# Moving the output clearings, the stores' steps and the sign copies around the sigmoid sets of a WKV and binary-FFN kernel

## The chip, the cores and the metric

The kernel runs on one core of a Trainium2 chip. The metric is device time of one launch in microseconds (us). The engines are called PE (TensorE), DVE (VectorE), ACT (ScalarE), POOL (GpSimd) and SP (SyncE); a "line" such as L963 is a line of the kernel before.

## What is computed

For x and k of shape (4, 1024, 1024), batch, time, channel:

```
ek = exp(min(k, 30)); ekv = ek * k
forward and backward scans over time, with a decay per channel and batch, of ekv and of ek
den = df + db - ek + exp(min(u + k, 30));  num likewise with ekv
out = sigmoid(x) * num / max(den, 1e-8) * (0.8 + 0.2 * tf)
y   = out @ (sign(weight) * mean|weight|).T + bias
result = x + y
```

tf is a sigmoid of the sum of a batch's condition row.

## The kernel before, in words

**Tiles and steps.** The work is cut into N = 32 tiles, one per batch and group of 128 channels, each 128 channels by 1024 times in float32. There are 32 steps, n = 0 to 31; every engine has its own program with a `step(n, ...)` of its own, and semaphores tie them together. LAST is 24 (the last batch's first tile), SOON is 26 and LAG is 9.

**One tile's way through the engines.** PE turns k and x into channel-major form (`k_turn`, `s_turn`). ACT makes the exponentials (`exps`, L655 to L659). DVE multiplies (L939, L942), scans four times (L911 forward twice, L925 backward twice), adds up the denominator (L963, both tensor inputs in SBUF), and forms `gate` of the tile before (L954: wkv times sigmoid). The reciprocal takes a chain over two engines: ACT `inverse` (L690, L692), POOL L379 (semaphore `chk`), ACT L755 (`two`), POOL L385 (`inv`). DVE's gate of step n waits for `inv` of tile n-1. POOL multiplies the gated value with the numerator (`base`, L362), ACT splits it in a high and a low half (`halves`, L699 and L701), and POOL L342 writes the low half (`lo`) that PE's products use. POOL's order in a step is base(n-2), a store if one is due, chk(n-1), lo(n-2), inv(n-1), the numerator's accumulating DMA L388, and at step 28 and later a second store if one is due.

**Sigmoid sets.** Sigmoids need another activation table, so ACT does three x tiles at once in every third step (L796, with a table load before and after, L796 and L802). Six further x tiles lie in `x_end`; before, one of them is done in each sigmoid step from 9 on (L801).

**Products, clearings and stores.** For the first three batches an output tile m is made in two halves, unit u = 2m and 2m+1, of 16 matmuls each (`unit`, L466). ACT clears a unit from PSUM (`evac`, L669), PE turns it back to time-major form (`turned`, L468), and ACT copies it into one of four buffers `o_nat[m % 4]` (`y_copy`, L678). `clear(lo, hi)` does `evac(u)` and `y_copy(u-1)` for its units. POOL then adds tile m to the output with an accumulating DMA (`store`, L355). `y_copy(2m)` waits until `store(m-4)` has landed, since it writes the same buffer:

```
if h == 0 and m >= NO:
    act.wait_ge(o_out[m % NO], m // NO * 16)
```

**Two tables set the order.** `made(n)` says how many units PE has made by step n (`MORE` holds exceptions), `cleared(n)` how many ACT has cleared (`CLEARED` holds exceptions). From `cleared` follows the step of every store: one step after its second half is copied, one store per step, two from step 28 on:

```
n = copied[2 * m + 1] + 1
while added.count(n) >= (2 if n >= N - 4 else 1) or added and n < added[-1]:
    n += 1
```

**A step right behind a sigmoid set** (n % 3 == 1, up to 22) is "hasty": ACT does the halves before any clearing. In steps 0 to 7 ACT also prepares the weight's signs (absolute sum, sign, and the copy into `sgn`, L806). From step 26 on PE does `s_turn` first; steps 30 and 31 and the tail do the last batch in time-major form (`begun`, `across`, L488), with the results scaled on DVE (L1025 to L1035).

## Time and profile before

| | us |
|---|---|
| median of 3 runs | 514.82 |
| lowest and highest run | 514.12 and 516.09 |
| the profiled execution's own time | 513.96 |
| its span in the trace | 512.1 |
| VectorE busy | 482.4 (94%) |
| ScalarE busy | 411.1 (80%) |
| GpSimd busy | 381.1 (74%) |
| TensorE matmul busy | 354.7 (69%) |

The span is the trace's own length; the execution's time has 1.9 us more around it. All places below are given in us from the span's start. A busy engine is not yet a bound engine: an instruction that is held up inside counts as busy.

### The profile page before, as it was taken

The numbers are of one execution on the slowest core, as the hardware profiler recorded it, in microseconds if no ns is written. First come the engines' busy times: TensorE is split into PE (matmuls) and PEld (weight loads), VectorE is DVE, ScalarE is ACT, GpSimd is POOL, SyncE is SP. The second block draws the span as 40 slices with busy tenths as digits, with TensorE's granted clock in tenths as the row PEclk, the third lists the DMA queues.
The fourth block names the chain that finished last, engine by engine and source line by source line (L and its number), as shares of the span: only waits on it lengthen the run. The fifth ranks groups of instructions, "written<-read, shape, count | busy, mean of one in ns | idle before, by whom it ended". The sixth has DMA issues, their size and how long they took to land.

```text
span 512.1 us, 5399 instructions
## 1 busy us (share of the span) xinstructions
PE 354.7 (69%) x1803; PEld 209.6 (41%) x1803; DVE 482.4 (94%) x346; ACT 411.1 (80%) x459; POOL 381.1 (74%) x210
## 2 busy tenths in 40 slices
PE   3322223332288876877688698788849999999996
PEld 2212222332244443444254354355425555544442
DVE  6999998999999999999999999989999999999666
ACT  3978998898889879988988988898698888894500
POOL 0067769848777886888689678869778889999483
PEclk9996656555687998889898889979788999999999
DMA  8877999999997989598798957879866559995368
GB/s 216 228 213 241 256 224 234 293 314 242 265 245 188 204 194 165 142 200 190 161 199 190 205 83 209 162 164 206 165 114 90 108 102 150 193 153 78 42 113 217
DMA packets 101283, 94.22 MB, mean 184 GB/s; under 512 B 2924, under 2 KB 93064, under 8 KB 100744
## 3 DMA queue, kind: packets, MB, share of 16 engines
q0 software_dynamic: 31440, 36.18, 46.1%
q1 hardware_dynamic: 67720, 56.65, 35.1%
q10 hardware_dynamic: 2096, 1.05, 0.8%
q8 instruction: 15, 0.25, 0.2%
q14 instruction: 12, 0.10, 0.1%
HBM read 60.31 MB, written 37.75 MB: 191 GB/s over the span
## 4 chain that ended last, share of the span: by engine, by line
POOL 23%; ACT 23%; PE 22%; issue 16%; DVE 14%; DMA 0%; SPq 0%; DVEq 0%; ACTq 0%; POOLq 0%
POOL wkv L379 9%; PE prod L447 8%; DVE terms L925 4%; POOL acts L342 4%; DVE terms L911 4%; POOL wkv L385 4%; POOL out_dram L355 3%; PE prod L488 3%; ACT x_nat L796 3%; ACT rec L690 2%; ACT terms L655 2%; ACT euk L659 2%; ACT rec L692 2%; PE sT L488 2%; PE kT L488 2%
## 5 line engine op out<-in xcount | busy, mean ns | idle before, releaser
L447 PE MATMUL prod<-acts,sgn 128*128 128x512 f16 x752 | 180.2, 395 | 0.0
L925 DVE TENSOR_TENSOR_SCAN terms<-cols,y_start,terms 128x1024 f32<-128x1024 f32 x64 | 147.0, 2337 | 1.1
L911 DVE TENSOR_TENSOR_SCAN terms<-cols,terms 128x1024 f32<-128x1024 f32 x64 | 142.7, 2270 | 0.0
L447 PEld LDWEIGHTS prod<-acts,sgn 128*128 128x128 f16 x752 | 76.7, 102 | 86.6 <-issue 13.5
L362 POOL TENSOR_TENSOR wkv<-wkv,terms 128x1024 f32<-128x1024 f32 x31 | 73.4, 2367 | 50.7 <-DVE wkv L954 50.7
L379 POOL TENSOR_TENSOR wkv<-euk,rec 128x1024 f32<-128x1024 f32 x31 | 82.3, 2654 | 37.2 <-ACT rec L692 37.2
L385 POOL TENSOR_TENSOR wkv<-wkv,rec 128x1024 f32<-128x1024 f32 x31 | 81.8, 2639 | 1.2 <-ACT wkv L755 1.2
L342 POOL TENSOR_TENSOR acts<-wkv,rec 128x1024 f16<-128x1024 f32 x30 | 77.7, 2590 | 4.7 <-ACT rec L701 4.6
L422 PE MATMUL prod<-ident,o_nat 128*128 128x128 f16 x64 | 8.3, 311 | 72.8 <-ACT o_nat L790 72.8
L422 PE MATMUL kT<-ident,k_nat 128*128 128x128 f32 x248 | 45.9, 347 | 16.7 <-DVE own L942 16.5
L422 PE MATMUL sT<-ident,x_nat 128*128 128x128 f32 x208 | 38.0, 343 | 25.4 <-DVE wkv L954 16.7
L963 DVE SCALAR_TENSOR_TENSOR euk<-euk,terms 128x1024 f32<-128x1024 f32 x31 | 52.8, 1704 | 1.1
L755 ACT ACTIVATE wkv<-wkv 128x1024 f32<-128x1024 f32 x31 | 32.7, 1055 | 23.6 <-POOL wkv L379 23.6
L422 PE MATMUL yT<-ident,y_fm 128*128 128x128 f32 x192 | 31.2, 288 | 26.2 <-ACT o_nat L678 25.7
L388 POOL DMA_DIRECT2D terms<-own x32 | 35.8, 1120 | 17.4 <-DVE terms L925 17.2
L422 PEld LDWEIGHTS kT<-ident,k_nat 128*128 128x128 f32 x248 | 38.7, 184 | 23.7 <-issue 22.7
L422 PEld LDWEIGHTS sT<-ident,x_nat 128*128 128x128 f32 x208 | 31.3, 179 | 28.8 <-issue 16.3
L954 DVE SCALAR_TENSOR_TENSOR wkv<-wkv,sT 128x1024 f32<-128x1024 f32 x31 | 37.6, 1212 | 4.6 <-POOL wkv L385 4.6
L669 ACT ACTIVATE y_fm<-prod,bcol,oscale 128x512 f32<-128x512 f32 x47 | 36.1, 769 | 4.8 <-PE prod L447 2.7
L355 POOL DMA_DIRECT2D out_dram<-o_nat x24 | 39.9, 1662 | 0.0
L422 PEld LDWEIGHTS yT<-ident,y_fm 128*128 128x128 f32 x192 | 23.8, 148 | 38.9 <-ACT y_fm L669 32.7
L690 ACT ACTIVATE rec<-euk,lnb 128x1024 f32<-128x1024 f32 x31 | 35.7, 1151 | 4.5 <-DVE euk L963 4.4
(119 smaller groups left out, 587.0 us busy)
## 6 DMA issues: line engine op xcount, KB each, us to landing
terms<-own POOLq DMA_DIRECT2D x32, 512.0 KB, 5.2
out_dram<-in_x_dram SPq DMA_DIRECT2D x32, 512.0 KB, 7.2
k_nat<-in_fside_BxSxS_dram SPq DMA_DIRECT2D x30, 512.0 KB, 6.1
x_nat<-in_x_dram SPq DMA_DIRECT2D x26, 512.0 KB, 3.6
out_dram<-o_nat POOLq DMA_DIRECT2D x24, 512.0 KB, 8.0
y_fm<-in_L_ffn_weight_dram SPq DMA_DIRECT2D x8, 512.0 KB, 8.0
out_dram<-in_L_ffn_bias_dram POOLq DMA_DIRECT2D x8, 512.0 KB, 7.5
x_end<-in_x_dram SPq DMA_DIRECT2D x6, 512.0 KB, 8.9
```

The source lines that it names most:

```text
L342: pool.tensor_tensor(acts[:, 1, n % (2 * CT), :], wkv[p][:, :], rec[p][:, :], ALU.subtract)\
L355: pool.dma_start(tile_of(out, m), o_nat[m % NO][:, :, :], accum_op=ALU.add)\
L362: pool.tensor_tensor(wkv[n % 2][:, :], wkv[n % 2][:, :], ekv[n % NV], ALU.mult).then_inc(st["base"], 1)
L379: pool.tensor_tensor(W, euk[1 - p][:, :], R, ALU.mult).then_inc(st["chk"], 1)
L385: pool.tensor_tensor(W, W, R, ALU.mult).then_inc(st["inv"], 1)
L422: ins = pe.transpose(dst(q), what(q), one)
L447: ins = pe.matmul(made_in(u), view[:, c, m % CT * P:m % CT * P + P], acts[:, part, m // CT % 2 * CT + c, h * H:(h + 1) * H], start=(part = ...
L690: act.activation(rec[p][:, :], euk[p][:, :], ACT.Ln, bias=lnb[:, 0:1]).then_inc(st["ln"], 1)
L911: dve.tensor_tensor_scan(buf, d, buf, 0.0, ALU.mult, ALU.add).then_inc(st["F" + kind], 1)
L925: dve.tensor_tensor_scan(buf[:, ::-1], d, buf[:, ::-1], y_start[:, i:i + 1], ALU.mult, ALU.add)\
L954: dve.scalar_tensor_tensor(W, W, HI_SCALE * LO_GAIN / DEN_MIN, sT[:, :], ALU.min, ALU.mult)\
L963: dve.scalar_tensor_tensor(U, U, E30, E, ALU.min, ALU.add).then_inc(st["den"], 1)
```

## The change

Five things change. (1) In a sigmoid step from 9 to 21 only one unit is cleared (none in step 9); the other is cleared in the next step. `MORE` and `CLEARED` say so, and in such a step PE leaves out the last `turned` and does it in the next step, behind `k_turn`. (2) One unit more is made in steps 20 and 23, and one less in steps 19 and 22. (3) The copy of unit 31 (step 24) stands behind `two` instead of ahead of the halves. (4) The sign copy of step n moves to step n+1, behind `two`. (5) Of the six sigmoids in `x_end`, two are done in step 9 and one each in steps 12 to 21 (before, one each in steps 9 to 24), and their loads are issued in steps 2 to 7 instead of 4 to 9.

```diff
-    MORE = {19: 23, 20: 25, 21: 28, 22: 30, 23: 32, 24: 32, 25: 36, 26: 39, 27: 42, 28: 45}
+    MORE = {20: 25, 21: 27, 22: 29, 23: 32, 24: 32, 25: 36, 26: 39, 27: 42, 28: 45}
...
-    CLEARED = {23: 32, 25: 35, 26: 38, 27: 41, 28: 44, 29: 47}
+    CLEARED = {9: 0, 12: 6, 15: 12, 18: 18, 21: 25, 23: 32, 25: 35, 26: 38, 27: 41, 28: 44, 29: 47}
...
+    def turns(n):
+        return n % 3 == 0 and n < SOON
...
-                if 4 <= n < 10:
-                    sp.dma_start(x_of(SOON + n - 4), tile_of(x, SOON + n - 4)).then_inc(s_soon, 16)
+                if 2 <= n < 8:
+                    sp.dma_start(x_of(SOON + n - 2), tile_of(x, SOON + n - 2)).then_inc(s_soon, 16)
...
+                if turns(n - 1) and LAG < n < LAST:
+                    turned(units[0] - 2)
...
-                    turned(u - 1)
+                    if not turns(n):
+                        turned(u - 1)
...
-                hasty = low and n < LAST and n % 3 == 1
+                hasty = low and n < LAST and turns(n - 1)
...
-                if n == LAST:
-                    y_copy(4 * CT - 1)
                 if late and n < N - 2 and not hasty:
                     clear(cleared(n - 1), sooner)
...
+                if n == LAST:
+                    y_copy(4 * CT - 1)
                 if late and hasty:
                     clear(cleared(n - 1), sooner)
+                if 1 <= n <= CT:
+
+                    done(act, "wT", n - 1)
+                    act.mul(sgn[:, :, (n - 1) * P:n * P], wT, SIGN).then_inc(st["wTc"], 1)
...
-                    if n >= 9:
+                    for i in {9: (0, 1), 12: (2,), 15: (3,), 18: (4,), 21: (5,)}.get(n, ()):
 
                         act.wait_ge(s_soon, 16 * (N - SOON))
-                        i = SOON + n // 3 - 3
-                        act.activation(x_of(i), x_of(i), ACT.Sigmoid).then_inc(st["soon"], 1)
+                        act.activation(x_of(SOON + i), x_of(SOON + i), ACT.Sigmoid).then_inc(st["soon"], 1)
...
-                if wt:
-
-                    done(act, "wT", n)
-                    act.mul(sgn[:, :, n * P:(n + 1) * P], wT, SIGN).then_inc(st["wTc"], 1)
```

Evaluated, the two tables give these clearings and stores (steps that differ, and the last ones):

| step | cleared before | cleared now | store before | store now |
|---|---|---|---|---|
| 12 | 5, 6 | 5 | 1 | 1 |
| 13 | 7, 8 | 6, 7, 8 | 2 | none |
| 14 | 9, 10 | 9, 10 | 3 | 2 |
| 19 | 19, 20, 21 | 18, 19, 20 | 8 | 7 |
| 23 | 29, 30, 31 | 28, 29, 30, 31 | 12 | 11 |
| 27 | 38, 39, 40 | 38, 39, 40 | 16 | 15 |
| 28 | 41, 42, 43 | 41, 42, 43 | 17, 18 | 16, 17 |
| 29 | 44, 45, 46 | 44, 45, 46 | 19, 20 | 18, 19 |
| 30 | 47 | 47 | 21, 22 | 20, 21 |
| 31 | none | none | 23 | 22, 23 |

**First place: ScalarE, end of step 12 and start of step 13.** In the names a digit is a buffer's number; L669 is `evac`, L678 `y_copy`, L690 and L692 the `inverse` of tile 12. Before:

```order
L659 ACTIVATE euk1<-kT,ucol 128x1024
L669 ACTIVATE y_fm1<-prod,bcol,oscale 128x512
L678 COPY o_nat2<-yT 128x512
L796 ACT_TABLE_LOAD
L796 ACTIVATE x_nat0<-x_nat0 128x1024
L796 ACTIVATE x_nat1<-x_nat1 128x1024
L796 ACTIVATE x_nat2<-x_nat2 128x1024
L801 ACTIVATE x_end<-x_end 128x1024
L802 ACT_TABLE_LOAD
L690 ACTIVATE rec0<-euk0,lnb 128x1024
L692 ACTIVATE rec0<-rec0 128x1024
```

Now:

```order
L665 ACTIVATE euk1<-kT,ucol 128x1024
L806 ACT_TABLE_LOAD
L806 ACTIVATE x_nat0<-x_nat0 128x1024
L806 ACTIVATE x_nat1<-x_nat1 128x1024
L806 ACTIVATE x_nat2<-x_nat2 128x1024
L810 ACTIVATE x_end<-x_end 128x1024
L811 ACT_TABLE_LOAD
L696 ACTIVATE rec0<-euk0,lnb 128x1024
L698 ACTIVATE rec0<-rec0 128x1024
```

One clearing (two instructions) has left the place ahead of the table load; it stands in step 13 now, behind `exps`.

**Second place: GpSimd, from base(25) to the second store of step 28.** o_nat0 to o_nat3 are the four output buffers; tile m lies in buffer m % 4. Before:

```order
L362 TENSOR_TENSOR wkv1<-wkv1,terms 128x1024 [waits num_in1,d_gate]
L355 DMA out_0_dram<-o_nat0 128x8x128 [waits x_out2,d_yc]
L379 TENSOR_TENSOR wkv0<-euk0,rec0 128x1024 [waits d_lo,d_rec]
L342 TENSOR_TENSOR acts<-wkv1,rec1 128x1024 [waits d_hib]
L385 TENSOR_TENSOR wkv0<-wkv0,rec0 128x1024 [waits d_two]
L388 DMA terms<-own1 128x1024 [waits d_yn]
L362 TENSOR_TENSOR wkv0<-wkv0,terms 128x1024 [waits num_in0,d_gate]
L355 DMA out_0_dram<-o_nat1 128x8x128 [waits x_out2,d_yc]
L379 TENSOR_TENSOR wkv1<-euk1,rec1 128x1024 [waits d_lo,d_rec]
L342 TENSOR_TENSOR acts<-wkv0,rec0 128x1024 [waits d_hib]
L385 TENSOR_TENSOR wkv1<-wkv1,rec1 128x1024 [waits d_two]
```

Now, from base(26) on:

```order
L365 TENSOR_TENSOR wkv0<-wkv0,terms 128x1024 [waits num_in0,d_gate]
L358 DMA out_0_dram<-o_nat0 128x8x128 [waits x_out2,d_yc]
L382 TENSOR_TENSOR wkv1<-euk1,rec1 128x1024 [waits d_lo,d_rec]
L345 TENSOR_TENSOR acts<-wkv0,rec0 128x1024 [waits d_hib]
L388 TENSOR_TENSOR wkv1<-wkv1,rec1 128x1024 [waits d_two]
L391 DMA terms<-own0 128x1024 [waits d_yn]
L358 DMA out_0_dram<-o_nat1 128x8x128 [waits x_out2,d_yc]
L365 TENSOR_TENSOR wkv1<-wkv1,terms 128x1024 [waits num_in1,d_gate]
L358 DMA out_0_dram<-o_nat2 128x8x128 [waits x_out2,d_yc]
```

The store of o_nat0 (tile 16) has moved from step 27 to step 28, behind base(26), and that of o_nat1 (tile 17) from the start of step 28 to its end.

**Third place: ScalarE, start of step 28.** The same instructions before and now; those now are:

```order
L696 ACTIVATE rec1<-euk1,lnb 128x1024 [waits d_lo,d_den]
L698 ACTIVATE rec1<-rec1 128x1024 [waits d_ln]
L675 ACTIVATE y_fm0<-prod,bcol,oscale 128x512 [waits d_yT,d_prod,s_osc]
L684 COPY o_nat0<-yT 128x512 [waits d_yT,o_out0]
L705 ACTIVATE acts<-wkv0 128x1024 [waits d_prod,d_base]
```

The copy of unit 40 into o_nat0 (semaphore o_out0: tile 16's store has landed) stands ahead of the halves of tile 26, unmoved by the change.

## Rows read from the trace of the kernel before

**Rows 1.** Busy time of each engine: us (share of span), instructions.
```profile
PE 354.7 (69%) x1803; PEld 209.6 (41%) x1803; DVE 482.4 (94%) x346; ACT 411.1 (80%) x459; POOL 381.1 (74%) x210
```
**Rows 2.** Groups of instructions, DVE: xcount, busy us, mean ns, idle us before.
```profile
L963 DVE SCALAR_TENSOR_TENSOR euk<-euk,terms 128x1024 f32<-128x1024 f32 x31 | 52.8, 1704 | 1.1
```
**Rows 3.** What DVE waited for: us in total, times, longest.
```profile
DVE wkv L954 <- POOL wkv L385: 4.6, 3, 2.2
```
**Rows 4.** DVE's timeline, steps 4 to 22: start us, us.
```profile
75.37 1.72 DVE L963 SCALAR_TENSOR_TENSOR euk<-euk,terms 128x1024 f32<-128x1024 f32 x1
79.33 1.22 DVE L954 SCALAR_TENSOR_TENSOR wkv<-wkv,sT 128x1024 f32<-128x1024 f32 x1 [2.24 <-POOL wkv L385]
...
193.37 1.23 DVE L963 SCALAR_TENSOR_TENSOR euk<-euk,terms 128x1024 f32<-128x1024 f32 x1
...
207.29 3.28 DVE L963 SCALAR_TENSOR_TENSOR euk<-euk,terms 128x1024 f32<-128x1024 f32 x1
...
310.92 2.86 DVE L963 SCALAR_TENSOR_TENSOR euk<-euk,terms 128x1024 f32<-128x1024 f32 x1
...
344.78 1.22 DVE L954 SCALAR_TENSOR_TENSOR wkv<-wkv,sT 128x1024 f32<-128x1024 f32 x1 [2.25 <-POOL wkv L385]
```
**Rows 5.** POOL's timeline, steps 13 and 20.
```profile
202.51 2.35 POOL L379 TENSOR_TENSOR wkv<-euk,rec 128x1024 f32<-128x1024 f32 x1 [2.78 <-ACT rec L692]
...
207.14 2.34 POOL L385 TENSOR_TENSOR wkv<-wkv,rec 128x1024 f32<-128x1024 f32 x1
...
308.01 2.38 POOL L342 TENSOR_TENSOR acts<-wkv,rec 128x1024 f16<-128x1024 f32 x1 [1.42 <-ACT rec L701]
```
**Rows 6.** ACT's timeline, steps 3 and 12.
```profile
68.12 1.02 ACT L806 ACTIVATE sgn<-prod 128x1024 f16<-128x1024 f16 x1
...
192.42 0.77 ACT L669 ACTIVATE y_fm<-prod,bcol,oscale 128x512 f32<-128x512 f32 x1
...
193.68 1.28 ACT L796 ACT_TABLE_LOAD   x1
```
**Rows 7.** PE's timeline, steps 13 and 14.
```profile
208.12 4.71 PE L447 MATMUL prod<-acts,sgn 128*128 128x512 f16 x16
...
218.90 3.62 PE L447 MATMUL prod<-acts,sgn 128*128 128x512 f16 x16
```
**Rows 8.** POOL's timeline, steps 28 and 29.
```profile
419.81 1.59 POOL L355 DMA_DIRECT2D out_dram<-o_nat  x1
...
429.14 1.90 POOL L355 DMA_DIRECT2D out_dram<-o_nat  x1
```
**Rows 9.** ACT's timeline, step 28: inverse, copies of units 40 and 42.
```profile
419.26 1.06 ACT L692 ACTIVATE rec<-rec 128x1024 f32<-128x1024 f32 x1
...
421.21 0.58 ACT L678 COPY o_nat<-yT 128x512 f32<-128x512 f32 x1
...
430.97 0.58 ACT L678 COPY o_nat<-yT 128x512 f32<-128x512 f32 x1
```
**Rows 10.** DMA issues at 419 to 421: xcount, KB each, us to landing.
```profile
out_dram<-o_nat POOLq DMA_DIRECT2D x1, 512.0 KB, 6.3
```
**Rows 11.** DMA issues at 429 to 430, the same columns.
```profile
out_dram<-o_nat POOLq DMA_DIRECT2D x1, 512.0 KB, 8.2
```
**Rows 12.** Landing times of all transfers from or to o_nat.
```profile
DMA to landing us min/median/max: 6.0/8.0/11.5
```
**Rows 13.** DMA issues of the whole page, the plain x loads.
```profile
x_nat<-in_x_dram SPq DMA_DIRECT2D x26, 512.0 KB, 3.6
```
**Rows 14.** DVE's timeline, steps 28 and 30: L963 and two gates.
```profile
428.96 1.22 DVE L963 SCALAR_TENSOR_TENSOR euk<-euk,terms 128x1024 f32<-128x1024 f32 x1
430.11 1.21 DVE L954 SCALAR_TENSOR_TENSOR wkv<-wkv,sT 128x1024 f32<-128x1024 f32 x1
...
457.95 1.21 DVE L954 SCALAR_TENSOR_TENSOR wkv<-wkv,sT 128x1024 f32<-128x1024 f32 x1
```
**Rows 15.** ACT's timeline, step 30: the first parked result.
```profile
452.60 0.57 ACT L706 COPY acts<-prod 128x512 f32<-128x512 f32 x1
```

More of the change, by code:

```diff
@@ L791, in step @@
                        .then_inc(st["sgn"], 1)
-                if n % 3 == 0 and n < SOON:
+                if turns(n):
                     for i in range(n, min(n + 3, SOON)):
```

## The prediction, made blind

> **What bounds the kernel now.** I read the engines' busy time first. VectorE is busy 482.4 of 512.1 us [rows 1], so nothing is gained that doesn't shorten VectorE's own sequence. But the groups of instructions show that part of this is no work: L963 takes 1704 ns in the mean of its 31 [rows 2], and 1.23 us where nothing disturbs it [rows 4]. 31 times (1.704 - 1.225) is 14.8 us. The waits add 4.6 us for L954 (`gate`) behind GpSimd's L385 (`inv`) [rows 3].
>
> The timelines say where it goes. From one free L963 to the next it is 207.29 - 193.37 = 13.92 us [rows 4]. At 207.29 L963 takes 3.28, and GpSimd's L385 had begun at 207.14 and ran until 209.48 [rows 5]: L963, which reads two SBUF tensors, finished 1.09 after L385's end. So a step loses (end of L385) - (start of L963) - 0.13, here 2.06. In step 4 L385 came later still; there L963 took 1.72 and the gate waited 2.24 [rows 4], 2.8 us in all. All such losses together are 14.8 + 4.6 = 19.4 us, and that is the most that any cure of them can bring. They lie in the steps behind sigmoid sets (4, 7, 10, 13, 16, 19, 22), in step 20 (2.86 - 1.23 = 1.6 [rows 4]) and, with under 1 us each, in 24, 25 and 27. L385 is late since ScalarE is: L379 waited 2.78 us for `rec` [rows 5], which stands behind the sigmoids and table loads.
>
> For the rest the useful measure is the distance from a gate to L385. The next L963 starts 1.15 + 11.6 = 12.8 us after a gate starts; L385 takes 2.34 [rows 5], so it does no harm if it starts within 10.4 us of the gate.
>
> **The change, part by part.**
>
> *The clearing that leaves the sigmoid step.* From 192.42 to 193.68 it holds ScalarE 1.26 us [rows 6]. Without it `rec`, L379 and L385 all come 1.26 earlier: L385 ends at 208.22, and step 13 loses 0.8 instead of 2.06. Steps 13, 16 and 19: -3.8. In step 10 one more sigmoid of about 0.95 comes in for the clearing, so -0.3. Step 22 also gets rid of the clearing behind its sigmoid set: -2.0 of its 3.2 (its gate waited 2.25 [rows 4]).
>
> *What the following steps get for it.* In step 13 the turning of unit 6 now waits for its `evac` behind `two`. PE has idled over 5 us by then; the unit at 208.12, behind an idle of 3.6, took 4.71, the warm one at 218.90 took 3.62 [rows 7]. I take 4.7 for unit 8 and put it at 206.3 to 210.9. ScalarE has three units to clear in that step, waits for unit 8, and begins `inverse` of tile 13 at 212.1, some 3 us after its denominator. In step 14 it waits again, for unit 9 (214.8), then come the halves (to 218.1), L342 (to 220.5), L385: 11.2 us behind the gate, 0.8 too late. That is what step 20 shows already: L342 at 308.01 waited 1.42 for L701 [rows 5]. So 0.7 to 0.8 is newly lost in each of steps 11, 14, 17 and 23: +2.9. Step 20, which had this loss at 1.6, keeps 0.7: -0.9.
>
> *Units moved to 20 and 23.* In step 23 PE now has three units; unit 31 ends about 19.2 us after the gate, its clearing pushes `inverse` of tile 23 some 5.9 us back, and step 24 loses 2.2 instead of 0.9: +1.3. Unit 31's copy behind `two`, and one sigmoid less in step 24, save the small losses of 25 and 27: -0.5.
>
> *Sign copies.* One takes 1.02 us [rows 6] and leaves the place ahead of `inverse`. But it now delays `exps` in the step before a set, where ScalarE is held to GpSimd's base and L379, so the set starts later by as much. -0.75 in step 4, -0.1 in step 7.
>
> *Loads of x_end two steps earlier.* Used 90 us later: 0; at worst they push k's loads, +1.
>
> Sum up to step 27: -3.8 -0.3 -2.0 +2.9 -0.9 +1.3 -0.5 -0.75 -0.1 = **-4.2 us**. From above it is bounded by -19.4, from below by 0 if the new waits take back all.
>
> *The stores.* Step 13 has no store now, and one per step is the rule, so every later tile is stored a step later up to step 28. Up to unit 38 a copy into o_nat finds its store landed. Unit 40 doesn't. Store 16 is issued at 419.81 [rows 8], the slot of store 17 before, and that slot's transfer lands after 6.3 [rows 10]: 426.1. The copy of unit 40 stood at 421.21 [rows 9]. Queued behind it on ScalarE are the halves, `two`, `exps`. In the frame of before:
>
> - 426.1, copy 0.5, halves twice 1.1 (ScalarE's pass of 1024 is 1.06 [rows 9]): 428.8. L342 2.3, then L385, which is held up by the L963 that began at 428.96 [rows 14] as the one of step 4 was, 3.3: 434.5. The gate stood at 430.11 [rows 14]: +4.4.
> - Store 17 now follows L385 and L388: issued at 434.5 + 0.6 = 435.1, landing 8.2 as in the same slot [rows 8, 11]: 443.3. The copy of unit 42 stood at 430.97 [rows 9] and has `inverse` of tile 28 behind it. 443.3 + 0.5, inverse 2.2, clearing 1.1, halves 2.2, L342 and L385 4.7: 454.0.
> - Store 19 follows that L385: 454.6, landing 8.0 (the median [rows 12]) 462.6, copy of unit 46 and halves 2.7: 465.3; L342 2.3, L385 3.3: 470.9. The gate stood at 457.95 [rows 14]: +13.0.
> - `two` ends and the first parked copy starts at 466.3 against 452.60 [rows 15]: +13.7. PE waits for it and has the last batch's products in front of it without a pause.
>
> I take **+13.6**, and +1.0 for PE's slower matmuls after its idle stretches (4.71 - 3.62 = 1.1 once [rows 7]).
>
> Total: -4.2 + 13.6 + 1.0 = +10.4. The profiled execution took 513.96, so 524.4; the median of the runs is 0.86 above that execution: 525.2, rounded to **525**. Landings at the ends of 6.0 and 11.5 [rows 12] move the three stalls together by -4.5 and +12; the part up to step 27 by +4 and, if the new waits stay out, -5. The forecast's own range is 517 to 532.
>
> **Rivals.**
>
> *A, a store lands in time.* The plain x loads of the same 512 KB land after 3.6 us [rows 13]. If the stores did, unit 40's copy would wait 423.4 - 421.2 = 2.2, unit 42's some 2 and unit 46's nothing, +3 to +4 at the end, and with -4.2 the kernel stays at 514. For it: a plain transfer of the size does it. Against it: no transfer of o_nat landed under 6.0 [rows 12]. The Trainium skill (DMA: Bandwidth & Descriptors, section on the anatomy of one SWDGE DMA) gives about 2.0 us plus bytes over 436 GB/s; by that estimate a store would land after 3.2 us and the sum would end near 514 too. By that rule the trace disagrees, with 6.0 to 11.5 for these accumulating stores. Chance 0.09: no change.
>
> *B, faster.* The place is L963 behind L385 in steps 10 to 27. It decides itself at 10.4 us from gate to L385: if ScalarE, 1.26 us ahead at each set, stays ahead and PE doesn't hold up units 8 and 9, L385 gets in under that in every step and all of the 19.4 but the 4.2 left in steps 4 and 7 go: -15.2. With the stalls at their low end (13.6 - 4.5 = 9.1) and PE's 1.0 that is -5.1, so 510. Against: 1.26 is less than the 2.2 by which L385 must move. Chance 0.07: faster.
>
> *C, the change doesn't do what it says.* If the sets' x tiles landed late, the earlier table load would be waited away. They are loaded a step ahead and land in 3.6 [rows 13], so I see it as part of the range: +6, 531.
>
> **How the numbers follow.** Forecast and C 0.84, all slower; A 0.09; B 0.07. 0.5% (2.6 us) is about what a measurement of this kernel can tell from no change. Range 515 to 532: it leaves out B, half of A and the longest landings.
>
> **What would show it.** In the changed trace: ScalarE's copies L684 (old L678) waiting for a DMA in steps 28 and 30, three waits of 5 to 10 us in all 18 to 23; VectorE's gates of steps 28 to 30 late by 4, 10 and 13; the L963 behind steps 13, 16, 19 about 2.0 instead of 3.3, and those of 14, 17 near 2.0 instead of 1.2; the span up to step 27's L963 about 4 shorter. I am wrong if no copy waits for a store, or if the waits end without moving the gates.

## The result and the profile after

The changed kernel takes **528.45 us** (median of 4 runs, 527.65 to 530.26) against 515.46 for the kernel before on the same chip: 1.026 of its time, 95% interval 1.0223 to 1.0297. It is slower, by 13 us. The profiled execution took 530.26, with a span of 528.4 (before: 513.96 and 512.1), so in the traces the difference is 16.3 us, and that is what has to be explained below. Some 3 us of it belong to this pair of executions and not to the change: the changed kernel's profiled execution is the slowest of its four, and that of the kernel before lies 1.5 below its median.

In the changed file lines have moved: the denominator L963 is L968, the gate L954 is L959, `inv` L385 is L388, `lo` L342 is L345, `chk` L379 is L382, `base` L362 is L365, the store L355 is L358, `evac` L669 is L675, `y_copy` L678 is L684, the `inverse` is L696 and L698, the halves are L705 and L707.

Busy time of each engine in the changed kernel, beside [rows 1]:

```profile
PE 354.3 (67%) x1797; PEld 209.4 (40%) x1803; DVE 488.7 (92%) x346; ACT 411.1 (78%) x459; POOL 383.7 (73%) x210
```

The group of the denominator in the changed kernel (xcount, busy us, mean ns, idle before), beside [rows 2]:

```profile
L968 DVE SCALAR_TENSOR_TENSOR euk<-euk,terms 128x1024 f32<-128x1024 f32 x31 | 58.6, 1889 | 1.1
```

And what VectorE, ScalarE and TensorE waited for in the changed kernel (us in total, times, longest), beside [rows 3]:

```profile
PE yT L425 <- ACT o_nat L684: 35.8, 9, 8.3
...
ACT o_nat L684 <- DMA out_dram<-o_nat: 14.5, 3, 7.9
DVE wkv L959 <- POOL wkv L388: 14.1, 6, 4.6
```

The work is the same on every engine. VectorE is busy 6.3 us longer, of which the 31 denominators have 5.8 (58.6 - 52.8), and its gates wait 14.1 us instead of 4.6, another 9.5. Together that is 15.8 of the 16.3. ScalarE now waits for stores to land, 14.5 us in three waits; there was no such wait before.

**Where in the program.** The measure of the prediction, the time from one denominator to the next less 13.92 us, taken for each step of both traces from VectorE's timeline (us; steps not named lose under 0.1 in both):

| step | 4 | 7 | 10 | 11 | 13 | 14 | 16 | 17 | 19 | 20 | 22 | 23 | 24 | 25 | 26 | 27 | sum |
|---|---|---|---|---|---|---|---|---|---|---|---|---|---|---|---|---|---|
| before | 2.8 | 2.2 | 1.6 | 0 | 2.1 | 0 | 2.1 | 0 | 2.1 | 1.6 | 3.2 | 0 | 0.9 | 0.4 | 0 | 0.5 | 19.5 |
| changed | 2.3 | 2.2 | 1.4 | 2.4 | 0.9 | 2.4 | 0.9 | 2.0 | 0.9 | 1.9 | 1.0 | 1.8 | 1.9 | 0.2 | 0.2 | 1.6 | 23.8 |

Up to step 27 the changed kernel loses 4.3 us more in this pair of traces. The rest, 12.4 us, comes in steps 28 to 30: the first parked copy stands at 469.32 against 452.60 [rows 15], 16.7 later, and the last products are 16.7 later too.

**Steps 28 to 30.** ScalarE's timeline in the changed kernel, the copies of units 40, 42 and 46, and the halves behind the first (start us, us, what ended the idle time before it):

```profile
430.36 0.59 ACT L684 COPY o_nat<-yT 128x512 f32<-128x512 f32 x1 [4.76 <-DMA out_dram<-o_nat]
430.85 1.06 ACT L705 ACTIVATE acts<-wkv 128x1024 f16<-128x1024 f32 x1
...
446.91 0.59 ACT L684 COPY o_nat<-yT 128x512 f32<-128x512 f32 x1 [7.90 <-DMA out_dram<-o_nat]
...
465.83 0.59 ACT L684 COPY o_nat<-yT 128x512 f32<-128x512 f32 x1 [1.83 <-DMA out_dram<-o_nat]
```

GpSimd's timeline in the changed kernel, the stores of tiles 16, 17 and 19 and the instructions that the first wait holds up:

```profile
424.09 1.60 POOL L358 DMA_DIRECT2D out_dram<-o_nat  x1
...
433.07 2.36 POOL L345 TENSOR_TENSOR acts<-wkv,rec 128x1024 f16<-128x1024 f32 x1 [4.99 <-ACT rec L707]
435.39 3.34 POOL L388 TENSOR_TENSOR wkv<-wkv,rec 128x1024 f32<-128x1024 f32 x1
...
439.28 1.90 POOL L358 DMA_DIRECT2D out_dram<-o_nat  x1
...
458.25 1.91 POOL L358 DMA_DIRECT2D out_dram<-o_nat  x1
```

VectorE's gates of steps 28, 29 and 30 in the changed kernel, beside [rows 14]:

```profile
438.76 1.22 DVE L959 SCALAR_TENSOR_TENSOR wkv<-wkv,sT 128x1024 f32<-128x1024 f32 x1 [2.25 <-POOL wkv L388]
...
457.73 1.22 DVE L959 SCALAR_TENSOR_TENSOR wkv<-wkv,sT 128x1024 f32<-128x1024 f32 x1 [4.57 <-POOL wkv L388]
...
474.23 1.21 DVE L959 SCALAR_TENSOR_TENSOR wkv<-wkv,sT 128x1024 f32<-128x1024 f32 x1
```

Read them together. From a store's issue to the copy that waits for it is 430.36 - 424.09 = 6.3 us, then 446.91 - 439.28 = 7.6, then 465.83 - 458.25 = 7.6. The store leaves only behind `inv`, the copy stands ahead of the halves, and the halves lead to the next `inv`: each wait makes the next store late, and so the next wait.

**Steps 13 and 14.** VectorE's timeline in the changed kernel:

```profile
208.97 2.13 DVE L968 SCALAR_TENSOR_TENSOR euk<-euk,terms 128x1024 f32<-128x1024 f32 x1
211.02 1.21 DVE L959 SCALAR_TENSOR_TENSOR wkv<-wkv,sT 128x1024 f32<-128x1024 f32 x1
...
223.80 1.23 DVE L968 SCALAR_TENSOR_TENSOR euk<-euk,terms 128x1024 f32<-128x1024 f32 x1
227.28 1.22 DVE L959 SCALAR_TENSOR_TENSOR wkv<-wkv,sT 128x1024 f32<-128x1024 f32 x1 [2.26 <-POOL wkv L388]
```

TensorE's timeline in the changed kernel, the held-back turning of unit 6 and the products of units 8 and 9:

```profile
207.76 1.09 PE L425 MATMUL yT<-ident,y_fm 128*128 128x128 f32 x4 [6.01 <-ACT o_nat L684]
208.64 5.56 PE L450 MATMUL prod<-acts,sgn 128*128 128x512 f16 x16
214.03 0.60 PE L425 MATMUL yT<-ident,y_fm 128*128 128x128 f32 x4
214.47 3.62 PE L450 MATMUL prod<-acts,sgn 128*128 128x512 f16 x16
```

ScalarE's timeline there in the changed kernel: the held-back clearing, the wait for unit 8, the `inverse` of tile 13:

```profile
206.38 0.76 ACT L675 ACTIVATE y_fm<-prod,bcol,oscale 128x512 f32<-128x512 f32 x1
207.04 0.57 ACT L684 COPY o_nat<-yT 128x512 f32<-128x512 f32 x1
...
214.28 0.78 ACT L675 ACTIVATE y_fm<-prod,bcol,oscale 128x512 f32<-128x512 f32 x1 [2.26 <-issue]
214.96 0.58 ACT L684 COPY o_nat<-yT 128x512 f32<-128x512 f32 x1
215.43 1.16 ACT L696 ACTIVATE rec<-euk,lnb 128x1024 f32<-128x1024 f32 x1
```

GpSimd's timeline in step 14 of the changed kernel:

```profile
221.55 2.37 POOL L345 TENSOR_TENSOR acts<-wkv,rec 128x1024 f16<-128x1024 f32 x1 [1.42 <-ACT rec L707]
223.88 3.37 POOL L388 TENSOR_TENSOR wkv<-wkv,rec 128x1024 f32<-128x1024 f32 x1
```

The profile puts ScalarE's wait of 2.26 to `issue`, which means that it shows no releaser; the unit that is cleared next ended on TensorE at 214.20, 0.1 us before.

Behind the sigmoid set the denominator takes 2.13 instead of 3.28 [rows 4], which is the gain of the change. In the next step `inv` starts at 223.88, 12.9 us behind the gate of 211.02, and the gate after it waits 2.26. The loss has moved one step on, and grown: 0.9 + 2.4 for steps 13 and 14 against 2.1 before.

**How far one trace can be read.** The changed kernel and e1 below are the same program up to step 19, and still step 11 loses 2.4 in the one and 1.5 in the other, and step 14 2.35 and 1.89. TensorE's timeline, the first products of step 10, in the changed kernel and in e1:

```profile
163.00 6.18 PE L450 MATMUL prod<-acts,sgn 128*128 128x512 f16 x16
...
163.09 5.33 PE L450 MATMUL prod<-acts,sgn 128*128 128x512 f16 x16
```

The granted clock is 0.58 over the first and 0.68 over the second, the products end 0.9 us apart, and so does everything behind them. In step 13 the products take 5.56 and 5.14. In the same way step 10 of e2, which lies ahead of its only edit, loses 2.5 where the kernel before loses 1.6. So a difference of up to 1 us in one step of two traces need not come from an edit. The larger ones, and those that stand in several runs, can be read.

### The profile page after: what moved, and what is told of

Same layout as the page of the kernel before. It is cut to its first block, busy times and chain, and to the rows that moved or that the text cites. A ratio compares the mean times of both kernels' runs of the same rounds, so it can differ in the third digit from the quotient of the medians.

```text
span 528.4 us, 5393 instructions
## 1 busy us (share of the span) xinstructions
PE 354.3 (67%) x1797; PEld 209.4 (40%) x1803; DVE 488.7 (92%) x346; ACT 411.1 (78%) x459; POOL 383.7 (73%) x210
## 4 chain that ended last, share of the span: by engine, by line
PE 29%; ACT 28%; POOL 16%; issue 13%; DVE 9%; DMA 4%; SPq 0%; ACTq 0%; DVEq 0%; POOLq 0%
PE prod L450 15%; POOL wkv L382 7%; DMA out_dram<-o_nat 4%; POOL wkv L388 4%; ACT x_nat L806 3%; PE prod L491 3%; DVE terms L930 3%; PE yT L425 3%; DVE terms L916 2%; ACT terms L661 2%; ACT rec L696 2%; ACT euk L665 2%; ACT L811 2%; ACT L806 2%; POOL acts L345 2%
## 5 line engine op out<-in xcount | busy, mean ns | idle before, releaser
L450 PE MATMUL prod<-acts,sgn 128*128 128x512 f16 x752 | 182.7, 399 | 0.0
L365 POOL TENSOR_TENSOR wkv<-wkv,terms 128x1024 f32<-128x1024 f32 x31 | 75.5, 2435 | 50.5 <-DVE wkv L959 50.5
L382 POOL TENSOR_TENSOR wkv<-euk,rec 128x1024 f32<-128x1024 f32 x31 | 79.5, 2565 | 39.2 <-ACT rec L698 39.1
L345 POOL TENSOR_TENSOR acts<-wkv,rec 128x1024 f16<-128x1024 f32 x30 | 73.9, 2464 | 17.5 <-ACT rec L707 17.3
L388 POOL TENSOR_TENSOR wkv<-wkv,rec 128x1024 f32<-128x1024 f32 x31 | 80.1, 2583 | 1.2 <-ACT wkv L759 1.2
L968 DVE SCALAR_TENSOR_TENSOR euk<-euk,terms 128x1024 f32<-128x1024 f32 x31 | 58.6, 1889 | 1.1
L425 PE MATMUL kT<-ident,k_nat 128*128 128x128 f32 x248 | 43.8, 335 | 16.3 <-DVE own L947 16.3
L675 ACT ACTIVATE y_fm<-prod,bcol,oscale 128x512 f32<-128x512 f32 x47 | 36.3, 772 | 21.6 <-issue 14.6
L425 PE MATMUL sT<-ident,x_nat 128*128 128x128 f32 x208 | 36.0, 330 | 24.8 <-ACT x_nat L806 16.8
L959 DVE SCALAR_TENSOR_TENSOR wkv<-wkv,sT 128x1024 f32<-128x1024 f32 x31 | 37.6, 1213 | 14.1 <-POOL wkv L388 14.1
L425 PEld LDWEIGHTS yT<-ident,y_fm 128*128 128x128 f32 x192 | 25.0, 152 | 52.8 <-ACT y_fm L675 35.6
L391 POOL DMA_DIRECT2D terms<-own x32 | 31.8, 994 | 17.2 <-DVE terms L930 17.1
L684 ACT COPY o_nat<-yT 128x512 f32<-128x512 f32 x48 | 27.8, 579 | 19.3 <-DMA out_dram<-o_nat 14.5
L358 POOL DMA_DIRECT2D out_dram<-o_nat x24 | 41.1, 1740 | 1.3 <-ACT o_nat L684 1.3
```

The source lines that it names most:

```text
L345: pool.tensor_tensor(acts[:, 1, n % (2 * CT), :], wkv[p][:, :], rec[p][:, :], ALU.subtract)\
L358: pool.dma_start(tile_of(out, m), o_nat[m % NO][:, :, :], accum_op=ALU.add)\
L365: pool.tensor_tensor(wkv[n % 2][:, :], wkv[n % 2][:, :], ekv[n % NV], ALU.mult).then_inc(st["base"], 1)
L382: pool.tensor_tensor(W, euk[1 - p][:, :], R, ALU.mult).then_inc(st["chk"], 1)
L388: pool.tensor_tensor(W, W, R, ALU.mult).then_inc(st["inv"], 1)
L425: ins = pe.transpose(dst(q), what(q), one)
```

## The experiments

Each is set against the kernel before on the same chip (medians of before: 515.58 for e1 to e4, 514.91 for f5 to f8, 515.18 for g1 to g4). Runs of different groups ran on different chips and are compared by these ratios.

| run | what it is | median us | ratio to before, 95% |
|---|---|---|---|
| changed kernel | | 528.45 | 1.026 (1.0223 to 1.0297) |
| e1 | changed, stores back in their steps | 516.52 | 1.001 (0.9993 to 1.0028) |
| e2 | before, stores late only | 528.04 | 1.0239 (1.0218 to 1.026) |
| e3 | e1, eviction ahead of the halves | 512.78 | 0.9945 (0.9926 to 0.9965) |
| e4 | before with parts 3, 4, 5 | 513.78 | 0.9972 (0.9957 to 0.9986) |
| f5 | e1, whole clearing ahead of the halves | 509.33 | 0.9887 (0.9856 to 0.9918) |
| f6 | e1, unit 29 back in step 22 | 517.04 | 1.0038 (1.0019 to 1.0056) |
| f7 | e4, low half behind `inv` | 512.73 | 0.9943 (0.9925 to 0.996) |
| f8 | e3, low half behind `inv` | 513.91 | 0.9979 (0.9957 to 1.0001) |
| g1 | f5, low half behind `inv` in steps 4, 7 | 508.99 | 0.9877 (0.9853 to 0.99) |
| g2, g3, g4 | before with part 4, 3 or 5 alone | 514.88, 514.40, 514.49 | one run each |

### The stores: taken out of the change, and put alone into the kernel before

e1 is the changed kernel with room for two stores in step 20, so that every store from tile 9 on has the step it had before:

```diff
-        while added.count(n) >= (2 if n >= N - 4 else 1) or added and n < added[-1]:
+        while added.count(n) >= (2 if n >= N - 4 or n == 20 else 1) or added and n < added[-1]:
```

> The changed kernel with one edit: two stores may be issued in step 20, so that from tile 9 on every store is in the step where it was before. Theory S (the one-step delay of the stores makes ScalarE's copies wait in steps 28 and 30, which the trace after shows as 14.5 us of DMA waits and 12.0 us more between VectorE's step 27 and the last gate): the waits vanish, and about 12 us with them: 516 to 519 us, the DVE steps up to 27 as in the changed kernel. Rival R (the copies of steps 28 to 30 would be late in any case, since ScalarE and TensorE come out of step 27 late): the time stays above 523 us, with other waits in place of the DMA's.

e2 is the kernel before with the stores of tiles 2 to 16 a step late and nothing else:

```diff
-        n = copied[2 * m + 1] + 1
+        n = max(copied[2 * m + 1] + 1, m + 12 if 2 <= m <= 16 else 0)
```

> The kernel before with one edit: stores 2 to 16 are issued one step later, as in the changed kernel; clearings, products and sign copies are as before. Theory S: the same three DMA waits, 526 to 529 us. Rival R (the delay hurts only in company with the other parts): under 521 us.

Measured: e1 516.52, no difference from before that can be told; e2 528.04, the changed kernel's time to half a microsecond. What ScalarE's copies waited for in e2:

```profile
ACT o_nat L678 <- DMA out_dram<-o_nat: 15.1, 4, 8.1
```

and its first two waits, on ScalarE's timeline:

```profile
427.89 0.59 ACT L678 COPY o_nat<-yT 128x512 f32<-128x512 f32 x1 [4.87 <-DMA out_dram<-o_nat]
...
444.63 0.59 ACT L678 COPY o_nat<-yT 128x512 f32<-128x512 f32 x1 [8.08 <-DMA out_dram<-o_nat]
```

In e1 these waits are gone. VectorE's timeline in e1, steps 28 to 30, for the rows of [rows 14]:

```profile
431.66 1.22 DVE L968 SCALAR_TENSOR_TENSOR euk<-euk,terms 128x1024 f32<-128x1024 f32 x1
432.81 1.21 DVE L959 SCALAR_TENSOR_TENSOR wkv<-wkv,sT 128x1024 f32<-128x1024 f32 x1
...
459.50 1.22 DVE L968 SCALAR_TENSOR_TENSOR euk<-euk,terms 128x1024 f32<-128x1024 f32 x1
```

459.50 - 431.66 is 27.84, two steps of 13.92 without a loss. So the stores' late steps cost 12 us in the medians, taken away (528.45 - 516.52 = 11.9) as well as added alone (528.04 - 515.58 = 12.5). This is shown, from both sides.

### What the other parts do together

e4 is the kernel before with the sign copies, unit 31's copy and the last sigmoids and their loads as in the change, but with its own clearings, units and stores (parts 3 to 5 of the diff above).

> The kernel before with the three parts of the change that don't touch the clearings' tables: sign copies a step later behind two, unit 31's copy behind two, and the x_end sigmoids and loads as in the changed kernel. Theory: the sign copies give 0.5 us in step 4 (2.83 before, 2.33 after) and nothing in step 7; unit 31's copy gives 0.9 us in step 24; the x_end sigmoids cost 1 us in step 10 and give 1 us or less in steps 24 and 25: together 1 us faster than before, 514 to 515 us. Rival (the sign copies' place carries what the change gains): 511 to 513 us.

Measured 513.78, ratio 0.9972: 1.4 us faster by the ratio, 1.8 by the medians. e1 has all five parts and the stores in place, and takes 516.52. What lies between, 2.7 us, is the price of parts 1 and 2 together, the clearings and the units, with the later stores of tiles 2 to 8 that follow from them. The clearings were meant to leave the sigmoid step, and apart from the stores they cost more than they bring.

### The held-back turning

Two theories stood for why the loss comes back a step later: the turning of the held-back unit, ahead of the products on TensorE, makes unit 8 late, and with it ScalarE's `inverse`; or ScalarE simply has as much to do as before, and the place matters little. e3 does the eviction ahead of the halves and leaves the copy behind `two`:

```diff
                 hasty = low and n < LAST and turns(n - 1)
+                if late and hasty:
+                    evac(cleared(n - 1))
                 if hasty:
...
-                if late and hasty:
-                    clear(cleared(n - 1), sooner)
+                if late and hasty and n > LAG + 1:
+                    y_copy(cleared(n - 1) - 1)
```

> The stores' cure of the run with stores moved back, and in each step behind a sigmoid set ScalarE clears the waiting unit (evac alone) ahead of the halves instead of behind the activation called two; the copy that goes with it stays behind. Theory M (the changed kernel's new losses of 1.8 to 2.4 us in steps 11, 14, 17, 20 and 23 come from the turning that TensorE holds back until that evac, and from the slow clock after its idle time): TensorE goes on some 4 us earlier, these five steps lose 0 to 1 us each, and the run is 6 to 10 us faster than the one with stores moved back alone: 508 to 512 us. Rival (the losses come from three clearings in one step, wherever they stand): 515 to 519 us, no gain over that run.

Measured 512.78, 3.7 us less than e1: a gain, and less of one than expected. TensorE's timeline in e3, the same turning:

```profile
205.18 1.08 PE L425 MATMUL yT<-ident,y_fm 128*128 128x128 f32 x4 [5.47 <-ACT o_nat L684]
206.06 4.74 PE L450 MATMUL prod<-acts,sgn 128*128 128x512 f16 x16
```

It still waits for the copy of unit 5: the turning writes `yT`, which that copy reads, and the copy (204.47, 0.57 us) now came last, 3 us behind the eviction. Counted from the denominator of step 12, the turning starts 12.2 us behind it against 12.7 in the changed kernel and in e1, so only 0.5 us sooner. f5 therefore takes the whole clearing, eviction of unit 6 and copy of unit 5, ahead of the halves:

```diff
+                if late and hasty:
+                    clear(cleared(n - 1), sooner_of(n))
                 if hasty:
                     done(act, "base", n - 2)
                     halves(n - 2, p)
...
-                if late and hasty:
-                    clear(cleared(n - 1), sooner)
```

with `sooner_of(n)` being `min(made(n - 1), cleared(n - 1) + 1)`.

> As the run with the early eviction, but in the steps behind a sigmoid set the whole held-back clearing (evictions of cleared(n-1) and the copy of unit cleared(n-1)-1) now goes ahead of the step's halves on ScalarE. Theory (the turning of the held-back unit waits for that copy too, 5.47 us in the run before, and so delays the units on TensorE): the turning starts some 3 us sooner, steps 14, 17, 20 and 23 lose about nothing instead of 0.6 to 1.1, the steps 13, 16, 19, 22 lose 1.8 instead of 1.3 since the halves come 1 us later; in all 511.5 to 512.5 us. Rival (the wait for the copy is hidden; only the halves count): 514 us or more.

Measured **509.33**, ratio 0.9887: 5.6 us faster than before, 2 us more than the theory gave; the interval is clear of no change. TensorE's timeline in f5:

```profile
202.06 0.72 PE L425 MATMUL yT<-ident,y_fm 128*128 128x128 f32 x4 [2.68 <-ACT o_nat L684]
202.57 5.26 PE L450 MATMUL prod<-acts,sgn 128*128 128x512 f16 x16
```

and VectorE's, steps 13 and 14:

```profile
206.78 3.00 DVE L971 SCALAR_TENSOR_TENSOR euk<-euk,terms 128x1024 f32<-128x1024 f32 x1
...
222.48 1.23 DVE L971 SCALAR_TENSOR_TENSOR euk<-euk,terms 128x1024 f32<-128x1024 f32 x1
```

Counted from the denominator of step 12 (192.87), the turning stands 9.2 us behind it instead of 12.7, 3.5 sooner; unit 8 is ready when ScalarE comes for it, and the denominator of step 14 is free: 1.23. Steps 14, 17, 20 and 23 lose nothing now. The price is a loss of 1.8 in step 13 again (the denominator takes 3.00), since the halves come behind the clearing. All losses up to step 27 are 15.0 us, against 19.5 before and 22.2 in e1. VectorE waits for `inv` in no step but the last, where it is 0.18. So it wasn't a matter of ScalarE's amount of work: the very same work, in another order, is 1.001 of the time before in e1 and 0.9887 in f5, some 6 us apart.

### The units of steps 22 and 23

```diff
-    MORE = {20: 25, 21: 27, 22: 29, 23: 32, 24: 32, 25: 36, 26: 39, 27: 42, 28: 45}
+    MORE = {20: 25, 21: 27, 22: 30, 23: 32, 24: 32, 25: 36, 26: 39, 27: 42, 28: 45}
```

> The changed kernel with the stores back in their former steps, and unit 29 made in step 22 again, so that step 23 makes two units and not three. Theory: the third unit of step 23 is what step 24 (1.93 us) and step 27 (1.59 us) lose by; they go to about 0.9 and 0.5, and the time from 516.5 to about 514.5. Rival: steps 22 and 23 lose as much more, since unit 29 is late in step 22 behind a held-back clearing: 516.5 us or above.

First a correction of what stands above under the change, part (2): by the table `MORE` the steps that make one unit less are 19 and 21, and not 19 and 22; step 22 makes two units in both kernels. So f6 does not restore the old table: its step 22 makes three units, 27 to 29, where before it made two, since unit 27 stays there.

Measured 517.04, no better than e1 (ratio 1.0038 against 1.001, intervals that meet); the rival had it right. VectorE's timeline in f6:

```profile
356.57 1.22 DVE L968 SCALAR_TENSOR_TENSOR euk<-euk,terms 128x1024 f32<-128x1024 f32 x1
362.36 1.22 DVE L959 SCALAR_TENSOR_TENSOR wkv<-wkv,sT 128x1024 f32<-128x1024 f32 x1 [4.57 <-POOL wkv L388]
```

Step 23 loses 4.65 instead of 1.6, and steps 24 and 25 nothing instead of 1.9 and 0.2. With unit 29 made in step 22, unit 28 is cleared in that step too, by the table. It is the second of three behind the held-back turning, and ScalarE waits 2.64 us for it ahead of the `inverse` of tile 22:

```profile
350.29 0.78 ACT L675 ACTIVATE y_fm<-prod,bcol,oscale 128x512 f32<-128x512 f32 x1 [2.64 <-issue]
...
351.43 1.16 ACT L696 ACTIVATE rec<-euk,lnb 128x1024 f32<-128x1024 f32 x1
```

In e1 the same wait of 2.64 stands one step later, for unit 31 and ahead of the `inverse` of tile 23. A third unit costs about as much in step 22 as in step 23, so this move is neither gain nor loss once part 1 is there. Part 2 without part 1 was not run.

### GpSimd's order

In f7 and f8 GpSimd makes `inv` ahead of the low half in the steps behind a sigmoid set:

```diff
-                if low:
+                behind = low and n < LAST and n % 3 == 1
+                if low and not behind:
                     low_half(n - 2, p)
                 if mid:
 
                     done(pool, "two", n - 1)
                     pool.tensor_tensor(W, W, R, ALU.mult).then_inc(st["inv"], 1)
+                if behind:
+                    low_half(n - 2, p)
```

> The kernel before with the signs, unit 31's copy and the last sigmoids as changed (513.8 us), and in the steps behind a sigmoid set GpSimd makes the reciprocal's part (wkv, L388 of the changed kernel) ahead of the low half. Theory: the gate of these steps waits 2.06 us each because that part stands last on GpSimd; with it first the loss goes to 1.1 or less in five steps, 507 to 510 us. Rival: the low half is then late for DVE's add by as much, and the step loses the same: 513 to 515 us.

> The early-eviction run (512.8 us) with the same order on GpSimd. Theory: 506 to 511 us, and the steps 13, 16, 19, 22 lose under 0.8 instead of 1.3. Rival: as in the run above, the low half is late and nothing is gained: 512 to 514 us.

Measured 512.73 and 513.91: the theory was wrong in both, and the rivals' times were right or nearly so. f7 gains 0.4 us on e4 by the medians and 1.5 by the ratios, intervals that just meet, and not 4 to 7. Its steps 13, 16 and 19 lose 1.0 instead of 2.1, as expected, but 14 and 17 now lose 1.2 where they lost nothing in the kernel before. In f8 steps 13, 16 and 19 lose nothing at all and 14, 17 and 20 lose 2.7 to 2.9. GpSimd's timeline in f8:

```profile
203.11 2.36 POOL L389 TENSOR_TENSOR wkv<-wkv,rec 128x1024 f32<-128x1024 f32 x1 [1.30 <-ACT wkv L764]
205.43 3.44 POOL L345 TENSOR_TENSOR acts<-wkv,rec 128x1024 f16<-128x1024 f32 x1
...
220.00 3.34 POOL L389 TENSOR_TENSOR wkv<-wkv,rec 128x1024 f32<-128x1024 f32 x1
```

The low half ends at 208.9 there, but unit 8's products do not wait for it: they start at 204.53, and need the low halves of tiles 0 to 7 alone. ScalarE waits 2.49 us for the unit, and the next `inv` starts at 220.00, 13.5 us behind its gate. Set beside e3, whose ScalarE and TensorE have the same order, the `inv` of step 14 starts 14.6 us behind the denominator of step 13 instead of 13.6, since unit 8's products took 5.78 us and not 4.74; and that denominator is no longer held up itself, so the gate behind it comes 1.3 us sooner. The chain over TensorE and ScalarE does not come sooner with it, and what was saved in step 13 is waited for in step 14. In the other direction the low half's lateness does show in f7: ScalarE's `inverse` waits 0.3 us for it in steps 10, 13, 16 and 22. Why f8's products were the slower ones in all three such steps (5.78, 5.64, 5.56 against 4.74, 5.12, 5.30 in e3) was not followed up.

g1 uses this order in steps 4 and 7 alone, where there are no products yet, on top of f5.

> The run with the whole clearing early (509.33 us), and GpSimd's low half behind the reciprocal's part in steps 4 and 7 alone. Where the low half was put last in all such steps, steps 4 and 7 lost 1.10 and the steps behind them 0.44, against 2.2 and nothing, a gain of 0.66 each. Theory: these two steps don't touch the rest, so 1.3 us less, 508.0 us. Rival: the order of the later steps shifts and gives it back, 509.3 us.

Measured 508.99 against f5's 509.33; the two intervals lie over each other, so the expected 1.3 us isn't there to be told. In its trace step 4 loses 1.1 and step 5 0.4, as expected, but step 7 lost 2.3 in this execution, where f8, with the same order up to there, lost 1.1.

### Parts 3, 4 and 5 one by one

Each alone in the kernel before, read by the steps' losses; the times themselves, one run each, are within 0.2% of before, which tells nothing.

> The kernel before with the signs' copies one step later and nothing else. Theory: steps 4 and 7 lose 2.2 each instead of 2.83 and 2.20, all other steps as before, 0.6 us less: the run is within 0.5% of before. Rival (the prediction's): step 4 gains 0.75 and step 7 0.1.

> The kernel before with unit 31's copy behind two turned units and nothing else. Theory: it touches only the last step, no step up to 27 loses other than before and the end moves by under 0.5 us. Rival: it is what took away the losses of steps 24 and 25 (0.91 and 0.40 us).

> The kernel before with the loads of the last x tiles two steps earlier and their sigmoids two in step 9 and one in steps 12, 15, 18 and 21. Theory: the sixth sigmoid leaves the set of step 24, so the losses of steps 24 and 25 (0.91 and 0.40) go to nothing, and comes into that of step 9, so step 10 loses 2.9 instead of 1.6: in sum nothing. Rival: step 10 stays at 1.6 and 1.3 us are gained.

| step | 4 | 7 | 10 | 20 | 22 | 24 | 25 | 27 |
|---|---|---|---|---|---|---|---|---|
| before | 2.8 | 2.2 | 1.6 | 1.6 | 3.2 | 0.9 | 0.4 | 0.5 |
| g2, signs | 2.2 | 2.2 | 2.5 | 0.5 | 3.3 | 0.9 | 0.4 | 1.4 |
| g3, copy of unit 31 | 2.8 | 2.2 | 1.6 | 1.6 | 3.3 | 0 | 0.5 | 0.8 |
| g4, last sigmoids | 2.9 | 2.2 | 2.7 | 0.5 | 3.3 | 0.9 | 0 | 0.5 |

The signs are worth 0.6 us in step 4 and nothing in step 7, as expected; every run with the signs moved and GpSimd's order left alone has 2.2 to 2.3 in step 4, every run without 2.8. The copy of unit 31 is what takes step 24's loss away, here and in e4; there the expectation was wrong and its rival right, for step 24 and not for 25. VectorE's timeline in g3:

```profile
371.44 1.23 DVE L963 SCALAR_TENSOR_TENSOR euk<-euk,terms 128x1024 f32<-128x1024 f32 x1
```

against 2.14 in the kernel before. The last sigmoids free step 25 only. Whether they bring 1.1 us into step 10 isn't shown: g2 loses 0.9 more there too, with nothing edited near it, and e2 likewise. Step 20 loses 1.1 us less in g2 and g4; the first products of step 19 took 3.6 us there and 5.3 in the kernel before and in g3. That is TensorE's pace, as above, and it is larger than the effects that are looked for.

## Why the prediction was right, and where it was not

Forecast: 525, range 515 to 532, slower with 0.84. Measured 528.45. The sign and the range hold, by the mechanism that was named. But of its two sums only one was right, and the other had the wrong sign. That the forecast came as near as 3 us is in part luck: errors of 8.5 and 2.2 us in the trace stand against each other. The direction is not luck, since the stores' 12 us alone carry it.

**The stores: right, a little high (+13.6 predicted, 12.4 in the trace, 12 by e1 and e2).** The table takes off the 4.3 us by which the changed kernel is behind when it leaves step 27, and is in the frame of before:

| | predicted | measured |
|---|---|---|
| landing of store 16, then the copy's wait | 6.3, 4.9 | 6.3, 4.76 |
| gate of step 28 | +4.4 | 438.76 - 4.3 - 430.11 = +4.3 |
| store 17 issued | 435.1 | 439.28 - 4.3 = 435.0 |
| issue to copy, store 17 | 8.2 | 7.6 |
| end of `inv` in step 29 | 454.0 | 455.34 + 2.35 - 4.3 = 453.4 |
| issue to copy, store 19 | 8.0 | 7.6 |
| gate of step 30 | +13.0 | 474.23 - 4.3 - 457.95 = +12.0 |
| first parked copy | +13.7 | 469.32 - 4.3 - 452.60 = +12.4 |

Two transfers landed 0.4 to 0.6 sooner than their slots of before, and in step 30 `inv` began before the denominator and took 2.37, not 3.3. The three waits are 14.5 us and not 18 to 23: the third is 1.83 only, since ScalarE itself was late by the two before it. The gates came within 1 us of where they were forecast, and they are what counts: a wait shrinks by what its engine is already late.

**TensorE's clock: +1.0 predicted, nothing came at the end.** The first parked copy is 16.7 later than before and so are the last products (520.81 against 504.09). Where the lower clock did cost is in steps 10 and 13, which the prediction had among its other terms.

**Up to step 27: -4.2 predicted, +4.3 measured in the trace. This is the step that failed.** The medians make it smaller, about +1: e1, which has all of the change but the stores' late end, takes 516.52 against 515.58. No measurement gives the forecast gain. By its terms, in the trace:

| term | predicted | measured |
|---|---|---|
| steps 13, 16, 19 | -3.8 | -3.5 |
| step 10 | -0.3 | -0.2 |
| step 22 | -2.0 | -2.3 |
| steps 11, 14, 17, 23 | +2.9 | **+8.5** |
| step 20 | -0.9 | +0.2 |
| step 24 | +1.3 | +1.0 |
| steps 25, 26, 27 | -0.5 | +1.1 |
| signs, steps 4 and 7 | -0.85 | -0.5 |

Every gain of the clearings' new place was sized right to 0.3 us. What they give back was not, and it is far above what two executions differ by (+6.8 in e1): "11.2 us behind the gate, 0.8 too late" was 12.9 us (211.02 to 223.88). The rule that a loss is what lies beyond 10.4 us held (12.9 - 10.4 = 2.5, and 2.4 was lost); the 11.2 that went into it was 1.7 short. Nor did it come as said there, with denominators near 2.0: that of step 14 took 1.23 with a gate that waited 2.26. Two things made the 1.7, both on TensorE, counted from the gate of step 12 (194.5 before, 196.19 in the changed kernel):

- The products of unit 8 were put at 206.3, 11.8 behind that gate. They started 12.45 behind it (208.64). The turning of the held-back unit was taken to wait for its eviction alone; it waits for the copy of unit 5 too, which stands behind the eviction, and starts only when that ends (207.04 + 0.57 = 207.61; 207.76). That is 0.7 us.
- The products took 5.56 us, not the 4.71 of the row they were sized by, 0.85 more. TensorE had been busy 2.2 of 9 us before, the granted clock was 0.50 there (the 1.2 GHz level) and 1.00 (2.4 GHz) only behind them. TensorE's windows in the changed kernel (stretch, us, PE busy, granted clock, DMA share, GB/s):

```profile
199.00:208.00 9.00, 2.18 (x10) 0.50 0.55 176
208.64:214.20 5.56, 5.56 (x19) 0.65 0.50 94
214.47:218.10 3.63, 3.63 (x20) 1.00 0.43 46
```

ScalarE waits for that unit and does the `inverse` behind it: 1.5 of the 1.7 us. About half of the 0.85 is this execution's: in e1 the same products took 5.14. That the unit's lateness is the cause is shown by e3 and f5, in which the turning comes 0.5 and 3.5 us sooner, counted from the denominator of step 12. ScalarE's wait for unit 8 goes from 2.26 (1.84 in e1) to 1.44 and to nothing, and steps 14, 17, 20 and 23 lose 3.8 us in e3, against 7.1 in e1, and nothing in f5. The clock adds to the loss where ScalarE already waits; where there is room it does no harm, as in f5, whose unit behind the turning was nearly as slow (5.26).

Steps 11, 14, 17 and 23 lose 8.5 us in the changed kernel and 6.8 in e1, whose clearings are the same. Of these 1.6 us steps 11 and 14 have 1.3, and there the two are one program, stores included: it is the pace of TensorE in one execution, and not the stores. The price of steps 25 to 27 (+1.1 instead of -0.5) lies in step 27, which took 1.6 in e1 as well and 0.5 in e3 and f5; that it hangs on the clearings is as far as the runs go.

Middle and tail were thus wrong by 8.5 in one direction and 2.2 in the other. The profiled execution came out 5.9 above its forecast (530.26 and 524.4), the median 3.2 above (528.45 and 525.2), since that execution was the slowest of the four. The stated range of 517 to 532 is narrower than its own terms: 525.2 with +12 for the landings and +4 for the middle is 541. The text says that it leaves out the longest landings; the measured time lies 3.5 below the stated end.

**The rivals.** A (a store lands in 3.6) is out: the landings in the changed kernel were these:

```profile
DMA to landing us min/median/max: 6.0/6.7/11.3
```

The estimate of 3.2 us that the Trainium skill allows (DMA: Bandwidth & Descriptors, anatomy of one SWDGE DMA) is out with it: the shortest landing is nearly twice as long. B (`inv` in time in every step from 10 on, so 15 us back) happened in no run: f5, the best for it, still loses 10.6 us in those steps. C is out: no sigmoid set waited for its x tiles.

## What to carry to other kernels

When work is taken out of a crowded step, follow the next consumer of its result on the in-order engine it was moved to: here a 1.3 us clearing, moved from ahead of the sigmoid set to behind `two` in the next step, held up a turning, the turning held up two units, and the units the very chain that was to be relieved. A step table that another table is derived from (clearings give the stores' steps) moves both; a shift by one did no harm here where buffers were free and cost 12 us where they weren't, so look at its last entries first. A loss that comes back in many steps can be attacked by order alone: f5 does exactly the work of the changed kernel and takes 509.33 us instead of 528.45. And before a difference of 1 us between two traces is given to an edit, look for it in steps where the two programs are the same.

## What the runs showed of the hardware

- VectorE's denominator, which reads two SBUF tensors, and GpSimd's tensor operations took turns, and the one that had begun stayed whole: `inv` at 223.88, 0.08 us behind the denominator, took 3.37 and left that one at 1.23, while in f5 `inv` began 0.4 us ahead (206.35, 2.35 us) and the denominator took 3.00. In the fourteen traces here a denominator that began while a GpSimd operation ran ended 1.07 to 1.16 us behind that one's end, whenever it had begun (176 cases), and a GpSimd operation that began inside a denominator ended 2.20 to 2.24 us behind that one's end (44 cases; where both begin within 0.05 us it goes either way). The time spent held up is inside the busy time of the instruction.
- Sixteen products of the same shape took 3.62 us at a granted clock of 1.00, 5.33 at 0.68 and 6.18 at 0.58, and a step of one and the same order of instructions differed by up to 1.2 us between two executions.
- The stores' landings moved little with their place in the program: 6.0 to 11.5 us before [rows 12], 6.0 to 11.3 after; the longest of all was 12.3, in e2.
